# Block rounding in a feed-forward layer: a minimum and a scaling read from the low halves of the raised numbers, in place of a subtraction and a minimum

## The reference

```python
def mx_quant(x):                                   # BLOCK = 32, BITS = 8
    xb = x.reshape(s[:-1] + (s[-1] // BLOCK, BLOCK))
    amax = jnp.max(jnp.abs(xb), axis=-1, keepdims=True)
    shared_exp = jnp.floor(jnp.log2(jnp.where(amax > 0, amax, 1.0)))
    scale = jnp.exp2(shared_exp - (BITS - 2))
    q = jnp.clip(jnp.round(xb / scale), -128, 127) * scale
...
h = mx_layernorm(x, ln_w, ln_b)                    # 1024 tokens x 256
h = bf16_round(mx_quant(h) @ mx_quant(W1).T + b1)  # 1024 x 1024
h = mx_gelu(h)
h = bf16_round(mx_quant(h) @ mx_quant(W2).T + b2)  # 1024 x 256
return bf16_round(residual + h)
```

## Time and profile before

| | |
|---|---|
| runs of the kernel before | 852.14, 853.74, 858.6 us (median 853.74) |
| span of the profiled execution | 856.9 us (the page has no other time of it) |
| this stage, first to last | 644.7 to 730.5 us |
| busy over the whole span | PE 636.9, DVE 637.5, ACT 357.3, POOL 203.5 us |

### The profile page before, as it was taken

The page is one execution under the profiler, slowest core; times in us unless marked ns, Lnnn a source line. Parts: engine busy times, 40 slices in busy tenths (PEclk is TensorE's granted clock), DMA queues, the critical chain, the costliest instruction groups (busy, mean ns, idle before and its releaser), DMA issues. The chain is left out here.

```text
span 856.9 us, 9591 instructions
## 1 busy us (share of the span) xinstructions
PE 636.9 (74%) x2846; PEld 400.6 (47%) x2849; DVE 637.5 (74%) x1324; ACT 357.3 (42%) x608; POOL 203.5 (24%) x203
## 2 busy tenths in 40 slices
PE   5769789999974537699747788988981685429991
PEld 3435445555544426467635455555450132325550
DVE  6799778968859887795556897978848988653434
ACT  4151847545413422545323656555622454403220
POOL 0000004434410000585550001010110255015651
PEclk9889989999987656799969898989985576559995
DMA  9500005655749024256210234242622500102225
GB/s 259 132 0 6 1 25 111 139 119 118 141 117 296 0 66 152 74 138 146 88 55 1 67 81 92 58 99 50 148 50 50 144 23 1 49 12 81 93 74 172
DMA packets 61687, 75.54 MB, mean 88 GB/s; under 512 B 16635, under 2 KB 42115, under 8 KB 60998
## 3 DMA queue, kind: packets, MB, share of 16 engines
q1 hardware_dynamic: 48470, 45.96, 19.1%
q0 software_dynamic: 13168, 28.97, 16.7%
HBM read 47.77 MB, written 10.36 MB: 68 GB/s over the span
## 5 line engine op out<-in xcount | busy, mean ns | idle before, releaser
L568 PE MATMUL ps<-hT,regA 128*128 128x512 f32 x256 | 118.3, 606 | 6.8 <-DVEq L665 6.1
L2007 PE MATMUL ps<-regA,regD 128*34 128x256 f32 x256 | 69.6, 396 | 14.6 <-DVE h L2133 10.7
L568 PEld LDWEIGHTS ps<-hT,regA 128*128 128x128 f32 x256 | 49.4, 194 | 60.4 <-issue 56.1
L581 PE MATMUL ps<-regA,regC 128*128 128x256 f32 x256 | 61.6, 384 | 3.2 <-DVE x L677 1.2
L581 PEld LDWEIGHTS ps<-regA,regC 128*128 128x128 f32 x256 | 47.0, 190 | 24.9 <-DVE regC L706 11.2
L754 POOL TENSOR_TENSOR regB<-regB,W1q 128x512 f32<-128x512 f32 x19 | 24.1, 1266 | 134.3 <-DVEq L696 134.3
L497 ACT ACTIVATE regC<-ps 128x512 f32<-128x512 f32 x32 | 19.0, 597 | 79.9 <-PE ps L568 79.8
L1854 ACT ACTIVATE regA<-ps 128x512 f32<-128x512 f32 x64 | 38.0, 596 | 30.8 <-PE ps L1993 29.9
L1807 POOL DMA_DIRECT2D yssm<-regC x13 | 15.6, 1201 | 136.4 <-DVE regC L2154 120.0
L693 DVE TENSOR_TENSOR_SCAN regB<-regB 128x512 f32<-128x512 f32 x38 | 44.5, 1212 | 4.0 <-DVE regB L686 3.6
L2113 DVE TENSOR_REDUCE regC<-ps 128x4 f32<-128x960 f32 x64 | 40.0, 683 | 7.2 <-PE ps L1957 7.2
(11 more groups left out here) (424 smaller groups left out, 1572.8 us busy)
## 6 DMA issues: line engine op xcount, KB each, us to landing
yssm<-regB POOLq DMA_DIRECT2D x19, 512.0 KB, 5.1
regC<-bc_rows SPq DMA_DIRECT2D x26, 256.0 KB, 3.7
yssm<-regC POOLq DMA_DIRECT2D x13, 512.0 KB, 6.9
W1q<-bc_rows SPq DMA_DIRECT2D x19, 256.0 KB, 3.2
regB<-in_L_w SPq DMA_DIRECT2D x4, 1088.0 KB, 11.7
y_rows<-regA SPq DMA_DIRECT2D x31, 128.0 KB
regB<-in_L_w SPq DMA_DIRECT2D x1, 2176.0 KB, 13.1
regC<-in_L_W SPq DMA_DIRECT2D x2, 1024.0 KB, 9.9
```

The source lines that it names most:

```text
L568: m = nc.tensor.matmul(ps[:, 2 + 2 * (u % 2) + j, :], w[:, k * 2048 + c * P:k * 2048 + (c + 1) * P], hT[:, k, hf * HALF:(hf + 1) * HALF], ...
L581: m = nc.tensor.matmul(ps[:, t // 2, (t % 2) * D:(t % 2 + 1) * D], itm[:, u % 2, t * P:(t + 1) * P], WDv[:, c // 2, c % 2, :], start=(c == ...
L2007: m = nc.tensor.matmul(ps[0:VW, 6 + j % 2, (n % 2) * S:(n % 2 + 1) * S], vaug[:, 2 * b + kt, hd, :], prob[:, n % 4, kt * S:(kt + 1) * S], ...
```

## The change

The step counts are read where raising left them: the low 16 bits of the raised float32 number, read as an int16, are the count of steps itself (its lower limit of -128 cannot be passed, since a step is at least 1/128 of the block's largest number). One operation takes the minimum with 127 and multiplies by the step, which `mx_unit_scales` keeps in `am[:, 2]` in place of the upper limit. The subtraction goes, on VectorE in the first half and on POOL in the second.

```diff
+        def mx_unit_scales(v, src, am):
...
+            v.link(nc.vector.tensor_scalar(am[:, 2, 0:n], am[:, 0, 0:n], 2.0 ** -100, 1 / 64, ALU.max, ALU.mult))
+
+        def mx_from_steps(dst, raised, am, s_done):
+
+            n = raised.shape[1]
+            steps = raised.bitcast(I16).rearrange("p n (k two) -> p n k two", two=2)[:, :, :, 0]
+            nc.vector.scalar_tensor_tensor(dst, steps, 127.0, mx_wide(am, 2, n), ALU.min, ALU.mult).then_inc(s_done, 1)
...
-                    def lower_hidden(t):
-                        pool.wait_ge(s_ra, t + 1)
-                        w = blocks(tmp2[:, t % 2, :])
-                        nc.gpsimd.tensor_tensor(w, w, mx_wide(am2[:, t % 2], 1, FF // BLK), ALU.subtract).then_inc(s_rs, 1)
...
-                    for i in range(NT + 3):
-                        if i < NT:
-                            lower_hidden(i)
-                        if i >= 3:
-                            add_first(i - 3)
+                    for t in range(NT):
+                        add_first(t)
...
-                        mx_scales(v, blocks(hbv[:, i]), am[:, i])
-                        mx_round(v, blocks(hbv[:, i]), blocks(q1v[:, i]), blocks(tmpv[:, i]), am[:, i], s_q1)
+                        mx_unit_scales(v, blocks(hbv[:, i]), am[:, i])
+                        v.link(nc.vector.tensor_tensor(blocks(tmpv[:, i]), blocks(hbv[:, i]),
+                                                       mx_wide(am[:, i], 1, 2 * D // BLK), ALU.add))
+                        mx_from_steps(blocks(q1v[:, i]), blocks(tmpv[:, i]), am[:, i], s_q1)
...
                     def limit_hidden(t):
-                        dve.wait_ge(s_rs, t + 1)
+                        dve.wait_ge(s_ra, t + 1)
                         if t >= 2:
                             dve.wait_ge(s_q2P, t - 1)
-                        mx_limit(blocks(q2[:, t % 2, :]), blocks(tmp2[:, t % 2, :]), am2[:, t % 2], s_q2)
+                        mx_from_steps(blocks(q2[:, t % 2, :]), blocks(tmp2[:, t % 2, :]), am2[:, t % 2], s_q2)
```

More of the change, by code:

```diff
@@ L1127, in mx_limit @@
             nc.vector.tensor_tensor(dst, tmp, mx_wide(am, 2, tmp.shape[1]), ALU.min).then_inc(s_done, 1)
-        def mx_round(v, src, dst, tmp, am, s_done):
+        def mx_unit_scales(v, src, am):
             n = src.shape[1]
-            v.link(nc.vector.tensor_tensor(tmp, src, mx_wide(am, 1, n), ALU.add))
-            v.link(nc.vector.tensor_tensor(tmp, tmp, mx_wide(am, 1, n), ALU.subtract))
-            mx_limit(dst, tmp, am, s_done)
+            v.link(nc.vector.tensor_reduce(am[:, 0, 0:n], src, AX.X, ALU.max, apply_absolute_value=True))
+            e = am[:, 0, 0:n].bitcast(I32)
+            v.link(nc.vector.tensor_scalar(e, e, 0x7F800000, None, ALU.bitwise_and))
+            v.mark(nc.vector.tensor_scalar(am[:, 1, 0:n], am[:, 0, 0:n], 2.0 ** -100, ROUND / 64, ALU.max, ALU.mult))
+            v.link(nc.vector.tensor_scalar(am[:, 2, 0:n], am[:, 0, 0:n], 2.0 ** -100, 1 / 64, ALU.max, ALU.mult))
[3 more added lines that the diff above has]
+            nc.vector.scalar_tensor_tensor(dst, steps, 127.0, mx_wide(am, 2, n), ALU.min, ALU.mult).then_inc(s_done, 1)
         s_w5 = ctx.enter_context(nc.semaphore("w5_loaded"))
@@ L2228, in stage5 @@
             (s_var, s_sd, s_nb, s_rb, s_var2, s_sd2, s_b, s_bc, s_v, s_q1, s_q1P, s_q1T, s_y1, s_y1b,
-             s_g1, s_ra, s_rs, s_q2, s_q2P, s_q2T, s_y2, s_y2b, s_z, s_x, s_bpart, s_brow, s_bsplit, s_var6, s_sd6) = (
-                sem("s5_" + n) for n in ("var sd nb rb var2 sd2 b bc v q1 q1P q1T y1 y1b g1 ra rs q2 q2P q2T y2 y2b z x "
+             s_g1, s_ra, s_q2, s_q2P, s_q2T, s_y2, s_y2b, s_z, s_x, s_bpart, s_brow, s_bsplit, s_var6, s_sd6) = (
+                sem("s5_" + n) for n in ("var sd nb rb var2 sd2 b bc v q1 q1P q1T y1 y1b g1 ra q2 q2P q2T y2 y2b z x "
                                          "bpart brow bsplit var6 sd6").split())
@@ L2423, in raise_hidden @@
                         g, w = blocks(g1[:, t % 2, :]), blocks(tmp2[:, t % 2, :])
-                        mx_scales(v, g, am2[:, t % 2])
+                        mx_unit_scales(v, g, am2[:, t % 2])
                         nc.vector.tensor_tensor(w, g, mx_wide(am2[:, t % 2], 1, FF // BLK), ALU.add).then_inc(s_ra, 1)
                     def limit_hidden(t):
-                        dve.wait_ge(s_rs, t + 1)
+                        dve.wait_ge(s_ra, t + 1)
                         if t >= 2:
                             dve.wait_ge(s_q2P, t - 1)
-                        mx_limit(blocks(q2[:, t % 2, :]), blocks(tmp2[:, t % 2, :]), am2[:, t % 2], s_q2)
+                        mx_from_steps(blocks(q2[:, t % 2, :]), blocks(tmp2[:, t % 2, :]), am2[:, t % 2], s_q2)
                     def result(t):
```

## The result

The kernel after takes 0.9937 of the kernel before, with a 95% interval of 0.991 to 0.9965; on the 857.5 us that the kernel before took in these 20 executions that is 5.4 us less, and the prediction said 5.7.

A forecast was written before the change was run, and what follows sets the result against it. VectorE bounds the first half and tiles 5 to 7, TensorE the tiles up to 4. A 3.1 us shift by tile 0, then shorter VectorE rounds, make 5.7 us: 853.74 - 5.7 = 848.0 us, range 844.0 to 852.5.

The forecast's parts named there:

- The pairs: First half, VectorE: each of four pairs loses a 512-wide subtraction of 0.73 us, 2.9 us in all.
- rival D: New limit on VectorE: int16 view read at double price, 2.29 us, stage ends where it did, 853.7 us; chance 0.06.
- Tile 0: First hidden tile on TensorE: transposed at 680.55 instead of 683.66, 3.1 us gained.
- Tiles 5 to 7: Last hidden tiles, VectorE the bound: without GpSimd's subtraction holding it, rounds fall from 6.09 to 4.9 us.
- the short addition's 0.46 us: Hidden tiles 5 to 7: GpSimd's remaining addition delays VectorE by 0.46 us for each of two rounds; range 0 to 0.67.
- The tail: Stage end: from tile 6's transpose to the last closing operation stays 10.3 us at the low clock.
- the rise of the clock moves with the string: Hidden tiles 0 to 4, TensorE: its clock rise shifts earlier by the same 3.1 us as the tiles.
- the low clock down as a rival: Hidden tiles, TensorE: clock does not rise in this stage at all, end 0.4 us later, 854.1 us; chance 0.09.

The follow-up runs named there:

- the hidden half alone: Kernel after with the four pairs' subtraction on VectorE put back, so only the hidden tiles read step counts; 0.9944 of the kernel before.
- the first four experiments: Run beside each other, ratios to the kernel before: pairs changed alone 0.9969, hidden tiles alone 0.9944, unused GpSimd subtractions added to the kernel after 0.9965, GpSimd zero writes instead 0.9944.
- the second measurement: Kernel after run once more without any edit, beside three other kernels on one chip; 0.9914 of the kernel before.
- the idle subtractions: Kernel after plus eight GpSimd subtractions of the old size on numbers nobody uses, started where the old ones started; 0.9965 of the kernel before.
- the fills: Kernel after plus GpSimd filling 2048 float32 numbers with zeros nobody reads, in place of unused subtractions; 0.9944 of the kernel before.
- the new order on TensorE alone: Kernel after with TensorE's first product of tile t + 3 put between tile t's transposes and its second product; 0.9898 of the kernel before.
- VectorE's order: Kernel after with each hidden tile limited right behind its raising: 0.998 of the kernel before; together with TensorE's changed order 0.9845.
- the fifty matmuls: 50 unread 512-column matmuls in TensorE's first-half pauses; added to the kernel after 0.9856 of the plain kernel before, added to the kernel before 0.9988.

## Why the prediction was right, point by point

**The pairs.** Four steps of 0.73 us; 2.89 measured. The int16 view of stride two costs what the float32 input cost, 0.69 and 1.22 us, as the nearest row had said; rival D is gone.

**Tile 0.** Predicted 3.1 us earlier. From the start of the first pair it is 677.38 - 652.44 = 24.94 us instead of 683.66 - 655.48 = 28.18: 3.2 us, the pairs' 2.89 and the wait of 0.27 us that closed.

**Tiles 5 to 7.** Rounds of 4.9 us were predicted and 4.85 measured, with the short addition's 0.46 us found as 0.41, on the closing operation. The mechanism is shown at the level of instructions: 2.13 us beside the old subtraction, 2.12 beside one whose result nobody waits for, 0.48 beside a fill. For the time of the stage the hold is worth nothing at the low clock (47.98 against 47.97 us). What it is worth where the clock rises rests on the hidden half alone, with the rounds at 4.85. Its 0.9944 may be in part the clock's, since 11 of its 12 executions have a mean granted clock of 0.84 or more and 19 of the 35 of the kernel before; among these the means are 854.0 and 856.1 us. That is 2.1 us where 2.6 was predicted, and the scatter allows about 0 to 4. The Trainium skill (SBUF — State Buffer, section Who interferes with whom) says that a VectorE instruction with two inputs in SBUF contends with a GpSimd instruction that reads SBUF and not with one that only writes; the runs agree, with 2.12 against 0.48 us.

**The tail.** From the transposes of tile 6 to the end of the last closing operation 10.3 us at the low clock were carried over from the old profile; 717.27 - 706.98 = 10.29 came out.

**The clock, where the step was wrong in kind and luck helped the number.** That "the rise of the clock moves with the string" does not hold. Counted from the start of the first pair, the rise came 696.2 - 655.5 = 40.7 us later in the profile of before, 682.8 - 652.4 = 30.4 in the first profile after, and never in the second. This is worth more than the change: 85.1 against 75.7 us for one and the same stage. In the first profile after, the stage's 7.5 us exceed the 5.7 by 1.8; I put most of that down to the earlier rise, since the pairs, tile 0, the rounds and the tail each came out within about 0.1 us of the forecast. I had put the low clock down as a rival with a chance of 0.09; the executions draw from both cases. The ratio came near the forecast because, of the executions of the kernel after that it counts, ten of eleven have a mean granted clock of 0.84 or more.

The executions show it. Each lists its mean granted clock over the whole kernel. This figure stands for the rise: without the added matmuls, the six profiles in which the clock rose in the hidden part have 0.842 to 0.853, the four in which it did not 0.828 or 0.829. I sorted the executions of the kernel after (20 and 12) and those of the kernel before that ran beside the first four experiments and beside the second measurement (35 and 29); the 20 did not run beside the 35. At 0.84 or more, 12 executions of after have a mean of 851.3 us and 26 of before 856.0: 4.7 less. Under 0.834, 18 of after have 863.1 and 26 of before 863.4: 0.3 less. So the change pays where the clock rises. The profiles say why it pays less where it does not: with 7.28 us for a tile TensorE is the bound, VectorE's shorter rounds end in a wait (1.1 us behind a held closing operation, 2.75 us behind a free one), and only the shift of the pairs is left to gain. How much of the pairs' 2.9 us is left then is not settled. Those 0.3 us pool measurements that did not run beside each other; beside the first four experiments the executions under 0.834 have means of 858.7 us with the idle subtractions (4) and 859.5 with the fills (6), both with the new pairs, against 862.8 of the kernel before (11).

A rival to the whole gain was not tested: that the change makes the rise rarer. Under 0.834 lie 18 of the 32 executions of after and 26 of the 64 of before. Over all executions the means are 856.5 against 857.8 us in the first measurement and 861.6 against 860.6 in the second, so that averaged over both cases no gain is shown. Nor is it settled what moves the rise: 22 and 28 matmuls in the pauses of the first half brought it there and did not keep it.

## What to carry to other kernels

Before pricing work taken off a second engine, look at what stands beside it on VectorE: here a GpSimd subtraction with two inputs, for whose result VectorE did not wait, held an unrelated operation of 0.48 us to 2.13 us. Then ask which engine is the bound there: the same hold cost nothing while TensorE took 7.28 us for a tile. Two engines with 4.62 and 4.85 us for a tile have to be improved together: with the new order on TensorE alone it waited up to 2.33 us for VectorE, and adding VectorE's order took another 7.0 us off at a mean granted clock of 0.84 or more. And where the clock of a stage rises in one execution and not in the next, one profile of before and one of after say little; sort the executions by the granted clock first, and count how many of each there are.

## What the runs showed of the hardware that was not expected

One and the same program had the hidden part at 2.4 GHz for 17 us in one execution and at 1.2 GHz throughout in another, with stages of 75.7 and 85.1 us. TensorE at the high level also fell back with only a short pause in its work. In the kernel after with the fifty matmuls, windows around tiles 0 to 2 (busy time and count of PE, PEld, DVE, ACT and POOL, then the granted clock, the DMA share and GB/s):

```profile
680.00:682.00 2.00, 0.90 (x11) 0.66 (x12) 1.41 (x3) 1.84 (x3) 0.00 (x0) 0.95 0.35 101
682.00:684.00 2.00, 2.00 (x9) 0.89 (x8) 1.97 (x4) 1.56 (x2) 0.00 (x0) 0.50 0.42 112
684.00:691.00 7.00, 5.90 (x24) 2.30 (x23) 4.71 (x8) 3.15 (x4) 0.67 (x1) 0.50 0.38 99
691.00:693.00 2.00, 2.00 (x6) 0.36 (x6) 1.90 (x5) 0.00 (x0) 0.00 (x0) 0.74 0.00 0
693.00:700.00 7.00, 4.79 (x37) 2.58 (x37) 5.36 (x9) 4.74 (x6) 0.67 (x1) 1.00 0.00 0
```

It falls at about 681.8, where TensorE has just had a wait of 1.10 us for ScalarE's copy, its only idle time from 680 to 684, stays at 1.2 GHz while TensorE is busy for 5.90 of 7 us, and is back at 2.4 GHz from about 692. The same wait of 1.10 us stands in tiles 2 and 3, at the high level. I can't say from these rows what tells the two apart. And an addition on GpSimd of 0.67 us cost VectorE 0.41 us: it ended late behind VectorE's limit, and VectorE's closing operation late behind it, so that the two engines handed the wait to and fro: 1.01 us, then 0.89.
